# Earlier placing of the row maxima and a looser mask wait for the value products, in a fused attention and top-2 expert kernel on one core

## What is computed

```python
Q = to_heads(x @ Wq); K = to_heads(x @ Wk); V = to_heads(x @ Wv)
scores = jnp.einsum('bhqd,bhkd->bhqk', Q, K) * scale
scores = jnp.where(causal_mask, jnp.asarray(-1000000.0, scores.dtype), scores)
weights = jax.nn.softmax(scores, axis=-1)
attn = jnp.einsum('bhqk,bhkd->bhqd', weights, V).reshape(b, s, D_OUT)
x = layernorm(x + attn @ Wo + bo)
...
xn = layernorm(x) * gamma + beta
combine, idx = top2_gate(xn, Wg)
out = sum over experts e of gate[e] * (gelu(xn @ W1[e] + b1[e]) @ W2[e] + b2[e])
x = layernorm(x + out)
```

## Time and profile before

| what | before |
|---|---|
| time, median of 3 runs | 984.21 us (983.76 to 986.77) |
| profiled execution, its own time | 991.02 us |
| its span, first to last instruction | 989.3 us |
| mean granted TensorE clock | 0.967 |
| PE busy | 854.8 us (86%) |
| DVE busy | 743.5 us (75%) |
| ACT busy | 677.1 us (68%) |
| POOL busy | 657.1 us (66%) |
| attention turns | about 40 us to 655 us of the span |

### The profile page before, as it was taken

The page is one execution under the profiler, slowest core; times in us unless marked ns, Lnnn a source line. Parts: engine busy times, 40 slices in busy tenths (PEclk is TensorE's granted clock), DMA queues, the critical chain, the costliest instruction groups (busy, mean ns, idle before and its releaser), DMA issues.

```text
span 989.3 us, 28895 instructions
## 1 busy us (share of the span) xinstructions
PE 854.8 (86%) x9151; PEld 564.2 (57%) x9151; DVE 743.5 (75%) x2021; ACT 677.1 (68%) x1433; POOL 657.1 (66%) x906
## 2 busy tenths in 40 slices
PE   4688898888989989989999988779999999999960
PEld 2334354444444444444444444349999989989950
DVE  1787778888988898889889889845554555377767
ACT  1277687777777777877877877746566555667863
POOL 6243555778777777787787786766767656567652
PEclk9799999999999999999999999979999999999985
DMA  7624635536446355355354342253233323276544
GB/s 197 196 69 158 176 93 163 161 106 206 127 146 211 97 171 174 96 166 158 93 185 129 112 153 73 61 143 83 79 85 88 85 72 96 78 248 181 170 128 139
DMA packets 168771, 132.37 MB, mean 134 GB/s; under 512 B 52845, under 2 KB 154516, under 8 KB 168496
## 3 DMA queue, kind: packets, MB, share of 16 engines
q1 hardware_dynamic: 156336, 112.34, 38.4%
q0 software_dynamic: 8640, 17.06, 5.1%
q10 hardware_dynamic: 3648, 1.12, 0.5%
HBM read 71.42 MB, written 61.01 MB: 134 GB/s over the span
## 4 chain that ended last, share of the span: by engine, by line
PE 39%; POOL 8%; issue 5%; ACT 5%; DVE 3%; DMA 2%; DVEq 0%; ACTq 0%; POOLq 0%; SPq 0%
PE ring L1241 14%; PE ring L1257 13%; PE ps_v L1177 3%; POOL probs L672 2%; PE ring L1114 2%; ACT probs L804 2%; POOL rs L738 1%; POOL rows_d L714 1%; PE ps_v L1231 1%; PE ring L1145 1%; DVE probs L1643 1%; PE ps_m L991 1%; DVE negmax L1301 1%; POOL qarea L636 1%; PE ps_m L1013 1%
## 5 line engine op out<-in xcount | busy, mean ns | idle before, releaser
L1301 DVE TENSOR_REDUCE negmax<-ring 128x2 f32<-128x1024 f32 (+3 forms) x512 | 407.5, 813 | 67.9 <-PE ring L1160 66.6
L804 ACT ACTIVATE probs<-ring 128x768 f32<-128x768 f32 (+1 forms) x384 | 334.8, 879 | 116.6 <-PE ring L1114 111.9
L672 POOL TENSOR_SCALAR_AFFINE_SELECT probs<-probs 128x512 f32<-128x512 f32 x256 | 162.4, 637 | 160.2 <-ACT probs L804 158.1
L928 ACT ACTIVATE vpad<-ring,b_s 128x128 f32<-128x128 f32 x568 | 162.2, 368 | 106.3 <-PE ring L1241 104.1
L722 POOL DMA_INDIRECT y_d<-vpad,xs x142 | 149.1, 1050 | 89.1 <-DVE vpad L1612 60.0
L1177 PE MATMUL ps_v<-probs,vpad 128*32 128x512 f32 (+3 forms) x2048 | 183.4, 448 | 10.4 <-POOL probs L672 10.4
L1257 PE MATMUL ring<-qarea,vpad 128*128 x1136 | 153.9, 279 | 3.4 <-issue 3.0
L1241 PE MATMUL ring<-vpad,w_t 128*128 128x128 f32 x1136 | 154.3, 280 | 2.8 <-issue 1.3
L714 POOL DMA_INDIRECT rows_d<-xn,slot x128 | 128.9, 1007 | 30.1 <-issue 27.1
L1241 PEld LDWEIGHTS ring<-vpad,w_t 128*128 128x128 f32 x1136 | 139.7, 194 | 5.7 <-issue 3.2
L1257 PEld LDWEIGHTS ring<-qarea,vpad 128*128 128x128 f32 x1136 | 137.8, 192 | 8.5 <-issue 7.0
(11 more groups left out here) (195 smaller groups left out, 1177.2 us busy)
## 6 DMA issues: line engine op xcount, KB each, us to landing
kside<-qk_d SPq DMA_DIRECT2D x32, 512.0 KB, 5.3
qk_d<-qarea SPq DMA_DIRECT2D x32, 384.0 KB, 2.7
xs<-rows_d SPq DMA_DIRECT2D x142, 66.0 KB, 1.9
qk_d<-qarea SPq DMA_DIRECT2D x32, 256.0 KB, 2.4
qarea<-qk_d SPq DMA_DIRECT2D x16, 512.0 KB
qodd<-qk_d SPq DMA_DIRECT2D x16, 512.0 KB
probs<-y_d SPq DMA_DIRECT2D x16, 512.0 KB, 5.1
xin<-L_attn_x SPq DMA_DIRECT2D x16, 256.0 KB, 3.9
```

What stands on the lines that cost most here:

```text
L672: pool.affine_select(out=diag, in_=diag, pattern=[[0, 4], [1, P]], compare_op=ALU.is_ge, fill=0.0, base=0, channel_multiplier=-1).then_inc ...
L804: nc.scalar.activation(of_unit(h // 2, part), ring[:, 2 * part % 3, :, (0, P, P)[part]:S], ACT.Exp, scale=SCALE).then_inc(sem("exp_done"), 1)
L928: ins = nc.scalar.activation(ht[:, n % 4, c, :], ps_a[:, n % 4, c * P:(c + 1) * P], ACT.Gelu_apprx_tanh, bias=b1_s[:, bass.ds(e, 1), c:c + ...
L1301: ins = nc.vector.tensor_reduce(negmax[:, n // 6 % 2, qb, s:s + 2], ring[:, (2 * n + 1) % 3, :, c0:c0 + nk], AX.X, ALU.max, negate=True)
```

## The change

Two things are edited. `place_max` is called at the start of steps 2, 6, 10 and 14, ahead of the step's first exponential, where it stood in the middle of the step. And the value products wait once per piece: the first two pieces for three of the group's four masks, the third piece for all four.

```diff
@@ body of ACT's program
                 for h in range(NH):
                     if h == 12 and i.exists(NB):
                         copy_u(act, i, 0)
+                    if h % 4 == 2:
+                        place_max(act, *((i, 1), (i, 2), (i, 3), (nxt, 0))[h // 4])
                     for u in range(3):
...
                         if u == 1:
                             middle(act, h, i, nxt, prev, rb)
-                            if h % 4 == 2:
-                                place_max(act, *((i, 1), (i, 2), (i, 3), (nxt, 0))[h // 4])
@@ values, in PE's program
                 if not b.exists(NB):
                     return
+                need(pe, sem("masked"), NH, b, GH * (g + 1) - (kbs[-1] < 2))
                 if kbs[0] == 0:
-                    need(pe, sem("masked"), NH, b, GH * (g + 1))
                     if g == 0:
```

## The result

The change is **slower**: 1006.86 us (1005.28 to 1010.04) against 985.49 us (983.76 to 991.31), a ratio of 1.020 with an interval of 1.017 to 1.024. The forecast was 999.0 in a range of 986 to 1008. The profiled execution of the changed kernel took 1007.93 us with a span of 1006.2; that of before had 989.3.

A forecast was written before the change was run, and what follows sets the result against it. No engine was full; handovers on the path round a turn (POOL's factors, ACT's chain, PE) bound the kernel. 23.9 + 0.4 - 6.2 - 1.8 - 1 - 0.5 = +14.8 us on 984.2 gave 999.0 us, range 986 to 1008.

The forecast's parts named there:

- The mask wait: PE's wait for POOL's mask at a turn's start, 0.67 us: removing it gains nothing a turn, transposes at most 0.11 earlier.
- what would release the 0.67: If ACT's chain behind POOL's factors were shorter by 0.67, the mask edit would bring 0.67 us a turn.
- The 0.5 behind the last turn: Behind the last turn no copy follows, so the mask edit may win 0.7 us once; counted as 0.5.
- The issue holds the next exponential by 0.68: On ACT, the moved DMA issue makes the exponential start 0.68 us after the maxima copy's end, with ACT empty meanwhile.
- Step 2, 0.68: In step 2 the exponential starts 0.68 us later; PE had no slack there and is 0.68 later.
- Step 6, 0.57: In step 6 the exponential moves by 0.77 us; PE has a slack of 0.20, so 0.57 more is felt.
- Steps 10 and 14, 0.46 and 0: Step 10's exponential moves 0.78 us, slack 0.32, so 0.46 more; step 14's moves 0.13, the following one 0.
- The sum of a full turn, 1.71: Losses of steps 2, 6, 10 and 14 together: 1.71 us a full turn, 23.9 over 14 turns.
- Turns 0 and 1, +0.4: Turns without the norm's work: exponentials behind the copies move about 0.1 us each, +0.4 for about four that PE feels.
- What comes back, -6.2: Scores' waits for the placing on PE, nine places in steps 4 and 8, all go: -6.2 us.
- Two slow-clock turns, -1.8: In turns 3 and 10, with PE's clock lowered, the change is worth -0.2 instead of +0.68 in step 2: -1.8 us.
- The clock rival: New idle times on PE bring four to seven more slow-clock turns: +6 to +10 us, 1005 to 1009; chance 0.12.

The follow-up runs named there:

- experiment 1: Only the value products' mask waits changed, placing left in place, against the kernel before: 1041.91 us against 1040.57, ratio 1.000.
- 6: Kernel before with the two normalized copies of step 1 moved to step 3 on ACT, mask waits as before: 985.75 us against 988.13.
- 7: Kernel before with step 1's two normalized copies moved to step 3 and the looser mask waits: 972.99 us in one run.
- Experiment 3: Kernel before with ACT's wait for its maxima copy put ahead of the exponential, DMA issue in its old place: 1040.85 us beside 1040.57.
- experiment 5: Kernel before with both edits, but the placing issued directly behind the step's first exponential: 983.01 us against 988.13, ratio 0.995.
- 4: Kernel before with the placing moved ahead of the exponential in step 6 only: 1058.41 us in one run, 18 us above the kernel before.

## Why the prediction was right, and where its sizes were off

- **Where it came out.** 1006.9 lies in the range, 1.1 from its upper end. No rival came: the issue was exposed, the exponentials behind all three copies cost their turn something, and the clock did not drop more often. The profiled execution took 1007.9 where 1005.8 was forecast.
- **The mask wait: nothing.** Right. The copy of the maxima lets 0.11 through, as forecast, and the time does not change (experiment 1). The sentence on what would release the 0.67 was right too (6, 7), and its size low: 0.88, since the wait also kept the value products from following the transposes closely. The 0.5 behind the last turn can't be read apart from the +0.21 of turn 15.
- **The issue holds the next exponential by 0.68.** Right: 28.0 us in 41 places. Experiment 3 splits it: 0.06 for the wait, the rest for the issue. DMA: Bandwidth & Descriptors of the Trainium skill (Issuing engines are not separate DMA queues), which the forecast quoted, calls the time of initiating a DMA usually small beside the DMA. In this kernel it cost nothing only where it lay beside running work, as in experiment 5; ahead of the exponential ACT lost 0.68.
- **Step 2, 0.68.** Right: 3.80 against 3.12.
- **Step 6, 0.57.** This term was mis-sized. It took the 0.20 between the exponential's end and the maxima products for slack. The rank product filled that time, and it stands behind the same wait, so the whole 0.78 was felt: the stretch from the copy of step 5 to that of step 9 grew by 0.80. Over 14 turns that is 3 us.
- **Steps 10 and 14, 0.46 and 0.** The stretch from the copy of step 9 to that of step 13 grew by 0.50, and from there to the next turn's copy by nothing. Right within 0.04.
- **The sum of a full turn, 1.71.** It was 1.96. That the total came within 2.1 us of the traces' 16.9 is in part luck. Over turns 2 to 13 the cost was 3.0 us larger than forecast (12 x 0.25), and 9.7 us came back instead of 7.6. Of these 9.7, the waits for the placing are 5.8 and the clock 1.5 (both below); the other 2.4 the forecast didn't have, and which waits they are stays open. Turns 14 and 15 cost 3.6 where 2.4 was forecast.
- **Turns 0 and 1, +0.4.** Less the 0.3 that the placing in turn 1 gives back, +0.1; it was -0.6. Why stays open.
- **What comes back, -6.2.** Right: all nine waits are gone. That an earlier issue alone does little is shown by experiment 5, where a DMA as early left nine waits standing, 4.5 us. The forecast had said that most would go merely because PE is late.
- **Two slow-clock turns, -1.8.** Wrong as a term. Turns 3 and 10 did come out at -0.19 and +0.42 instead of +1.96. But now turns 4 and 14 have such a stretch of lower clock (a granted clock of 0.75 and 0.66 over an eighth of the turn). Turn 4 takes 41.28 instead of 39.70, +1.6; turn 14, a short one, takes 40.40 where 37.00 + 1.96 = 38.96 was due, +1.4. So the saving was given back. Why it was these two turns is not shown.
- **The clock rival.** It did not come: turns 2 to 14 have two such stretches in either trace, and the mean clock is 0.967 in both.
- **The median.** The profiled spans differ by 16.9 where 14.8 was forecast. The medians of the runs differ by 21.4, and the interval of the ratio (16 to 24 us) holds the 16.9 at its lower end. The other 4.5 us lie in the step from the profile to the median, which the forecast had carried over: before, the median of the runs was 5.5 below the profiled execution (6.8 with the three runs of the forecast), after it only 1.1. The spread of the runs, up to 7.6 us, allows that; no run shows more of a cause.

## What to carry to other kernels

In this kernel a DMA issue on ACT's queue was an instruction of 0.6 us in front of whatever came next, and it was free only while something longer was already running there. So put it behind the instruction that starts that work, not ahead of it. Before taking away a wait, ask which other engine is held by the same producer: here PE (mask) and ACT (factors) both waited for one chain on POOL, either edit alone gave next to nothing (0.1 us or less), and both together gave 0.88 us a turn. A gap between a wait and the matmul that one looks at is slack only if no other instruction behind the same wait fills it.

## What was not expected

On two other chips the unchanged kernel took 1040.6 and 1047.9 us, where it took 985.5 and 988.1 on the others. On the one that was profiled (1047.9 us) PE's, DVE's and ACT's single instructions were equally long (the 1024-element exponential 1.02 us). A full turn was 38.9 instead of 37.75 us, and the exponential of step 4 started 5.20 us behind the placing's issue, where before it was 4.29:

```profile
511.02 0.61 ACTq L333 DMA_DIRECT2D qarea<-mt  x1
...
516.22 1.02 ACT L804 ACTIVATE probs<-ring 128x1024 f32<-128x1024 f32 x1 [1.39 <-PE ring L1114]
```

Experiments 1 and 4 have 5.1 to 5.3 there in most full turns. That would fit a later landing of the placing, but the scores' row (514.82, for 0.39 us) shows no wait for a DMA, and ACT starts 1.0 behind its end, so it stays open. So do the 50 us by which the part behind the turns was longer (383.0 against 332.8 us).
